# A short GpSimd instruction and a wait ahead of each scatter of two routings, in a kernel of graph layers, an LSTM and two expert layers

## The chip, the cores and the metric

The kernel runs on one core of a Trainium2 chip. The metric is the device time of one execution in microseconds (us). The core has five engines with a queue of instructions each: TensorE (PE), VectorE (DVE), ScalarE (ACT), GpSimd (POOL) and SyncE (SP, which here only starts DMAs). Engines wait for one another by semaphores alone.

## What is computed

The input `x` is 32 x 256 x 128 in fp32, 8192 tokens of 128 features, with a 256 x 256 adjacency matrix. Four residual layers follow one another, each behind a layer norm:

```python
x = x + _L0_gnn_ref(_layernorm(x), adj, adj, ...)    # gated graph layer
x = x + _L0_ffn_ref(_layernorm(x), ...)              # top-1 of 8 experts, behind a shared hidden layer of 512
x = x + _L1_gnn_ref(_layernorm(x), adj, ...)         # two graph layers, then LSTMs over windows of 1 to 4 nodes
x = x + _L1_ffn_ref(_layernorm(x), ...)              # top-2 of 8 experts, 341 wide
```

In the second layer `assign = argmax(probs)` chooses one expert for each token; in the fourth `top_k(probs, 2)` chooses two. The kernel computes only the chosen experts, so the tokens have to be brought into the order of the experts and back.

## The kernel before

The 8192 tokens are 64 tiles of 128 tokens. All layers run in one program with a stream of instructions written out for each engine.

**First routing (second layer).** The router runs over all 64 tiles (`b1_up`, PE line 1179, with ACT L828). In three batches (`PARTS`: 24, 24 and 16 tiles) DVE works out for each token its row in `sorted_in`, a DRAM array ordered by experts, and writes it to `dest_i` (L1767). `scatter_b(b)` on POOL then sends one indirect DMA per tile (L676), 128 rows of 512 bytes each. The first batch waits per scatter for an early count of the router's matmuls, which has been reached by then; the second batch waits likewise and from its 11th scatter on for the expert loop's matmuls (`b2_h`), 5 for each 8 scatters; the third for 7 of them for each 8 scatters.

**Expert loop (`b2_pe`).** The sorted rows are handled in groups of four tiles, 18 in all, with two buffers. SP loads a group (`b2_load`, L501); PE transposes it (L1142) one group ahead, computes the hidden layer (`hidden`, L1150, four matmuls of 512 columns, each counted in `b2_h`) and the chosen experts' output (L1291). SP may load groups 0 to 3 once the first batch of scatters has landed, groups 4 to 7 after the second, the rest after the third. `gather` on POOL (L704) brings the results back, also with one indirect DMA per tile. Ahead of each stands `pause()`, a memset of a 128 x 1 tile that nothing reads (L659), followed by a wait of POOL for the end of that memset.

**LSTM and second routing.** The third layer is done in two halves. In the second half the LSTM steps run (PE L1415 and L1422, ACT L975 and L983, DVE L2074 to L2090) while DVE works out the places for the first half's tokens; `scatter_d` then sends two indirect DMAs per tile for 32 tiles (L685, rows of 528 bytes into `expert_in`), each tile waiting for a step of the LSTM (`l_h`). When all 64 have landed, SP loads the first groups of the last expert stage (L537), and PE transposes them (L1432).

**Last stage.** PE computes the experts (L1442, L1452), POOL sends 64 more scatters for the second half's tokens (`rows_in`, L729) and 136 stores of result rows (`rows_home`, L710), and DVE adds the rows up. Neither of these has a pause.

POOL's order is fixed: the three batches of `scatter_b`, the gathers, layer norm statistics, `scatter_d`, then the last stage.

Of the kernel before, what the change touches and what calls it, by code (L numbers as in the profile page):

```python
# [55 lines left out]
def build(nc, x, adj_t, bias_io, gate_w, gate_b, w1, b1, wg, bg, wd, bd, g0_w, g0_b, g1_w, g1_b, wih_t, whh_t, bih, bhh,  # L56
# [30 lines left out]
    with ExitStack() as ctx:  # L87
# [494 lines left out]
        def _(pool):  # L582
            def step(ins):
                ins.then_inc(pool_step, 1)
                n_pool[0] += 1
                pool.wait_ge(pool_step, n_pool[0])
# [71 lines left out]
            def pause():  # L658
                step(pool.memset(pause_p[:, :], 0.0))  # L659

            def scatter_b(b):
                pool.wait_ge(rb.dest, b + 1)
                if b == 0:
                    pool.wait_ge(zeroed, ZEROS)
                lo, hi = PARTS[b]
                for t in range(lo, hi):
                    i = t - lo
                    if b == 0:
                        pool.wait_ge(rb.h, KH * NG // 2 + 7 + 3 * i // 4)
                    elif b == 1 and i < 10:  # L670
                        pool.wait_ge(rb.h, KH * NG - 9 + i)
                    elif b == 1:
                        pool.wait_ge(b2_h, 1 + 5 * (i - 10) // 8)
                    else:
                        pool.wait_ge(b2_h, 10 + 7 * i // 8)
                    pool.indirect_dma_start(  # L676
                        out=sorted_in, out_offset=bass.IndirectOffsetOnAxis(ap=dest_i[:, 0, t:t + 1], axis=0),
                        in_=XN[:, t, :], in_offset=None).then_inc(s_scat[0][b], 16)

            def scatter_d():  # L680
                pool.wait_ge(rd.dest, 1)
                for t in range(NH):
                    pool.wait_ge(l_h, NL + SCATTER_STEP + (NL - 1 - SCATTER_STEP) * t // NH)
                    for k in range(2):
                        pool.indirect_dma_start(  # L685
                            out=expert_in, out_offset=bass.IndirectOffsetOnAxis(ap=dest_i[:, k, t:t + 1], axis=0),
                            in_=XR[:, t, :], in_offset=None).then_inc(s_scat[1][0], 16)
# [26 lines left out]
            for b in range(len(PARTS)):  # L714
                scatter_b(b)
# [17 lines left out]
            for k in range(NGH // 2):  # L733
                t_finish(0, k, 2)
            scatter_d()
            for i in range(HOME_FIRST):
                if i in LN_AT:
# [1574 lines left out]
```

## Time and profile before

| | |
|---|---|
| median of 3 runs | 1147.16 us (1145.66 to 1150.82) |
| profiled execution | 1153.07 us, its span 1151.2 us |
| PE busy | 1024.0 us, 89% |
| ACT, DVE, POOL busy | 619.4 (54%), 600.0 (52%), 483.7 us (42%) |
| mean granted TensorE clock | 0.956 of full speed |
| software DMA queue (POOL's) | 12544 packets, 25.98 MB, 6.8% of 16 engines |

Times in rows are counted from the start of the span. "Busy" leaves out waits, branches and the issue of DMAs by SP. For an indirect DMA the busy time is POOL's part, the making of its descriptors, not the transfer. "Issue" is time in which an engine waited for nothing that the profile shows; "remote" or "another core or an unknown queue" is a release whose source the profile could not find.

### The profile page before, as it was taken

How to read it: one execution, taken by the hardware profiler on the slowest of the kernel's cores; microseconds unless marked ns; L12 is line 12 of the kernel's file. 1: busy time of each engine (PE TensorE's matmuls, PEld its weight loads, DVE VectorE, ACT ScalarE, POOL GpSimd, SP SyncE). 2: the span in 40 equal slices, each digit the busy share in tenths (PEclk: the TensorE clock that was granted, in tenths of full speed). 3: DMA queues.
4: the chain of work that ended last, by engine and by line, in shares of the span. 5: the costliest groups of instructions: out<-in, count | busy, mean ns of one | idle time of the engine just before them, and what ended most of it. 6: DMA issues, size and time to landing. Idle time of an engine off the chain costs nothing.

```text
span 1151.2 us, 17554 instructions
## 1 busy us (share of the span) xinstructions
PE 1024.0 (89%) x5432; PEld 715.8 (62%) x5433; DVE 600.0 (52%) x1829; ACT 619.4 (54%) x1158; POOL 483.7 (42%) x703
## 2 busy tenths in 40 slices
PE   5799967899989899999999996999897799989993
PEld 2344423577667544654785463448897798889893
DVE  6977874411174265655756753336464523333365
ACT  4678843444333485655338754456776555545551
POOL 5852274531634420000220075533536666656652
PEclk9899988799998999999999997999998999999997
DMA  9940012232323030000000011121122222212547
GB/s 274 365 193 1 1 50 69 87 97 70 97 71 86 28 116 0 1 1 0 1 1 1 1 48 40 41 61 31 43 62 65 64 81 65 82 62 66 189 164 223
DMA packets 79876, 86.28 MB, mean 75 GB/s; under 512 B 10115, under 2 KB 65971, under 8 KB 79027
## 3 DMA queue, kind: packets, MB, share of 16 engines
q1 hardware_dynamic: 67250, 59.28, 16.2%
q0 software_dynamic: 12544, 25.98, 6.8%
q8 instruction: 44, 0.72, 0.3%
q14 instruction: 38, 0.30, 0.1%
HBM read 40.64 MB, written 44.58 MB: 74 GB/s over the span
## 4 chain that ended last, share of the span: by engine, by line
PE 67%; DVE 13%; ACT 6%; issue 6%; another core or an unknown queue 6%; DMA 1%; ACTq 1%; POOL 1%; DVEq 0%; POOLq 0%; SPq 0%
PE bank L1415 17%; PE bank L1442 14%; PE bank L1422 9%; PE bank L1452 5%; PE bank L1150 4%; PE bank L1291 3%; PE bank L1331 2%; PE bank L1179 2%; PE bank L1359 2%; ACT sb_whh_sb L955 1%; PE bank L1348 1%; PE bank L1320 1%; PE bank L1340 1%; DVE sb_R L1542 1%
## 5 line engine op out<-in xcount | busy, mean ns | idle before, releaser
L1415 PE MATMUL bank<-sb_R,sb_wih_sb 128*128 128x512 f32 (+2 forms) x504 | 203.0, 554 | 15.0 <-ACT sb_R L975 7.6
L975 ACT ACTIVATE sb_R<-bank,sb_lb_sb 128x512 f32<-128x512 f32 (+2 forms) x252 | 153.2, 634 | 93.4 <-PE bank L1422 67.4
L710 POOL DMA_INDIRECT expert_out<-sb_R,sb_slot_row x136 | 132.6, 975 | 115.9 <-ACT sb_R L998 45.5
L2243 DVE TENSOR_TENSOR sb_R<-sb_R,bank 114x384 f32<-114x384 f32 x136 | 75.3, 554 | 181.9 <-ACT sb_R L1032 107.3
L1415 PEld LDWEIGHTS bank<-sb_R,sb_wih_sb 128*128 128x128 f32 x504 | 97.1, 194 | 113.7 <-issue 82.8
L1032 ACT ACTIVATE sb_R<-bank 114x384 f32<-114x384 f32 x136 | 66.4, 489 | 142.5 <-PE bank L1442 102.8
L1442 PE MATMUL bank<-sb_xt,sb_wih_sb 128*114 128x128 f32 x792 | 103.5, 282 | 22.8 <-issue 7.2
L1452 PE MATMUL bank<-sb_BIG,sb_R 114*128 x816 | 115.7, 278 | 0.7 <-DVE sb_R L2172 0.5
L1442 PEld LDWEIGHTS bank<-sb_xt,sb_wih_sb 128*114 128x114 f32 x792 | 94.1, 184 | 28.6 <-issue 25.4
L1422 PE MATMUL bank<-sb_R,sb_whh_sb 128*128 128x512 f32 (+2 forms) x288 | 111.1, 529 | 0.0
L685 POOL DMA_INDIRECT expert_in<-sb_R,sb_dest_i x64 | 64.4, 1007 | 105.1 <-DVE sb_dest_i L1767 62.7
L1452 PEld LDWEIGHTS bank<-sb_BIG,sb_R 114*128 114x128 f32 x816 | 103.5, 194 | 0.9 <-issue 0.9
L1442 PE MATMUL bank<-sb_xt,sb_whh_sb 128*114 128x128 f32 x792 | 98.6, 274 | 5.7 <-ACT sb_wih_sb L955 5.6
L614 POOL TENSOR_TENSOR sb_ln_p<-sb_ST 128x8 f32<-128x8 f32 (+2 forms) x15 | 3.3, 222 | 222.6 <-DVE sb_ST L1657 162.5
L1442 PEld LDWEIGHTS bank<-sb_xt,sb_whh_sb 128*114 128x114 f32 x792 | 91.2, 178 | 8.1 <-issue 7.1
L899 ACT ACTIVATE sb_R<-bank,sb_b_sb 128x512 f32<-128x512 f32 x72 | 47.9, 688 | 83.9 <-PE bank L1150 75.0
L1422 PEld LDWEIGHTS bank<-sb_R,sb_whh_sb 128*128 128x128 f32 x288 | 54.7, 190 | 50.5 <-issue 35.6
L676 POOL DMA_INDIRECT sorted_in<-sb_R,sb_dest_i x64 | 62.9, 983 | 44.2 <-issue 16.9
L729 POOL DMA_INDIRECT expert_in<-sb_R,sb_dest_i x64 | 61.9, 967 | 41.1 <-PE bank L1442 16.2
L1291 PE MATMUL bank<-sb_BIG,sb_R 128*128 x576 | 69.8, 279 | 8.3 <-issue 4.3
L1179 PE MATMUL bank<-sb_xt,sb_w_sb 128*128 128x512 f32 x128 | 68.5, 632 | 9.1 <-ACT sb_R L828 9.1
L1291 PEld LDWEIGHTS bank<-sb_BIG,sb_R 128*128 128x128 f32 x576 | 67.6, 195 | 9.4 <-issue 9.4
(308 smaller groups left out, 1690.9 us busy)
## 6 DMA issues: line engine op xcount, KB each, us to landing
sb_XS<-expert_in SPq DMA_DIRECT2D x17, 528.0 KB
expert_in<-sb_R SPq DMA_DIRECT2D x17, 512.0 KB, 6.1
sb_R<-expert_out SPq DMA_DIRECT2D x6, 1024.0 KB, 8.3
sorted_in<-sb_R SPq DMA_DIRECT2D x9, 512.0 KB, 5.4
sb_XS<-sorted_in SPq DMA_DIRECT2D x18, 256.0 KB
sorted_out<-sb_R SPq DMA_DIRECT2D x18, 256.0 KB
sb_X<-x SPq DMA_DIRECT2D x8, 512.0 KB, 7.4
out<-sb_X SPq DMA_DIRECT2D x6, 512.0 KB
```

Of the source, the lines that this page charges most:

```text
L676: pool.indirect_dma_start(out=sorted_in, out_offset=bass.IndirectOffsetOnAxis(ap=dest_i[:, 0, t:t + 1], axis=0), in_=XN[:, t, :], in_offse ...
L685: pool.indirect_dma_start(out=expert_in, out_offset=bass.IndirectOffsetOnAxis(ap=dest_i[:, k, t:t + 1], axis=0), in_=XR[:, t, :], in_offse ...
L710: pool.indirect_dma_start(out=expert_out, out_offset=bass.IndirectOffsetOnAxis(ap=slot_row[:, i:i + 1], axis=0), in_=yd[i // 8 % RING][:, ...
L975: act.activation(gb[s][k][:, 0:c], bank[4 * s + k][:, 0:c], funcs[k], bias=lb_sb[:, (p - 1) * GATES + k:(p - 1) * GATES + k + 1]).then_inc ...
L1032: act.activation(sl[j % 2][0:HC, :], bank[2 + 2 * (j % 2)][0:HC, 0:KU * P], ACT.Silu).then_inc(d2_silu, 1)
L1179: pe.matmul(bank[2 + c % 2][:, :], w1_sb[:, c * P:(c + 1) * P], xt[b // 2 % 2][:, b % 2 * BANK:(b % 2 + 1) * BANK], start=True, stop=True) ...
L1291: mm = pe.matmul(bank[6 + u][:, j * P:(j + 1) * P], Ht[u][:, c, j * P:(j + 1) * P], wd_sb[:, c, bass.ds(er[j] * D, D)], start=(c == 0 and ...
L1415: mm = pe.matmul(bank[4 * s + k][:, 0:c].rearrange("p (w b) -> p w b", b=GH), wih_sb[:, p - 1, k * P:(k + 1) * P], xin, start=True, stop=( ...
L1422: pe.matmul(bank[4 * s + k][:, 0:c], whh_sb[:, p - 1, k * P:(k + 1) * P], hst[s][:, 0:c], start=False, stop=True).then_inc(l_g, 1)
L1442: mm = pe.matmul(bank[2 + 2 * (j % 2) + part][0:HC, c * P:(c + 1) * P], weights_of(i)[:, part * UP + c * HC:part * UP + (c + 1) * HC], xt[ ...
L1452: mm = pe.matmul(bank[6 + j % 2][:, 0:D], hm[j % 2][0:HC, c * P:(c + 1) * P], down_sb[0:HC, bass.ds(expert * (KU * D) + c * D, D)], start= ...
L2243: dve.tensor_tensor(hm[j % 2][0:HC, :], sl[j % 2][0:HC, :], bank[3 + 2 * (j % 2)][0:HC, 0:KU * P], ALU.mult).then_inc(d2_m, 1)
```

## The change

`pause()` is called ahead of each of the 64 scatters of the first routing and of each of the 64 scatters of `scatter_d`. The gates stay where they are, ahead of the pause. `pause()` itself is unchanged.

```diff
@@ scatter_b
                         pool.wait_ge(b2_h, 1 + 5 * (i - 10) // 8)
                     else:
                         pool.wait_ge(b2_h, 10 + 7 * i // 8)
+                    pause()
                     pool.indirect_dma_start(
                         out=sorted_in, out_offset=bass.IndirectOffsetOnAxis(ap=dest_i[:, 0, t:t + 1], axis=0),
                         in_=XN[:, t, :], in_offset=None).then_inc(s_scat[0][b], 16)
@@ scatter_d
                 for t in range(NH):
                     pool.wait_ge(l_h, NL + SCATTER_STEP + (NL - 1 - SCATTER_STEP) * t // NH)
                     for k in range(2):
+                        pause()
                         pool.indirect_dma_start(
                             out=expert_in, out_offset=bass.IndirectOffsetOnAxis(ap=dest_i[:, k, t:t + 1], axis=0),
                             in_=XR[:, t, :], in_offset=None).then_inc(s_scat[1][0], 16)
```

What it calls:

```python
def step(ins):
    ins.then_inc(pool_step, 1)
    n_pool[0] += 1
    pool.wait_ge(pool_step, n_pool[0])

def pause():
    step(pool.memset(pause_p[:, :], 0.0))
```

## Rows read from the trace of the kernel before

**Rows 1.** The page: shares of the chain that ended last, by engine.
```profile
PE 67%; DVE 13%; ACT 6%; issue 6%; another core or an unknown queue 6%; DMA 1%; ACTq 1%; POOL 1%; DVEq 0%; POOLq 0%; SPq 0%
```

**Rows 2.** The chain in order of time, 164 to 176: start, us, what.
```profile
164.30 9.78 issue
```

**Rows 3.** Timeline, 142 to 185: start, us, engine, line, instruction [idle before <- releaser].
```profile
142.56 1.31 POOL L676 DMA_INDIRECT sorted_in<-sb_R,sb_dest_i  x1 [4.20 <-DVE sb_dest_i L1767]
...
173.13 0.95 POOL L676 DMA_INDIRECT sorted_in<-sb_R,sb_dest_i  x1 [0.30 <-issue]
...
174.08 0.69 ACT L828 ACTIVATE sb_R<-bank,sb_b_sb 128x512 f32<-128x512 f32 x1 [9.21 <-issue]
...
175.37 14.15 SPq L501 DMA_DIRECT2D sb_XS<-sorted_in  x3
...
184.95 0.97 POOL L676 DMA_INDIRECT sorted_in<-sb_R,sb_dest_i  x1 [10.86 <-DVE sb_dest_i L1767]
```

**Rows 4.** The chain in order of time, 194 to 210.
```profile
197.69 1.45 issue
```

**Rows 5.** Timeline of PE, 186 to 250: the first groups of the expert loop.
```profile
188.52 0.60 PE L1142 MATMUL bank<-sb_ident,sb_XS 128*128 128x128 f32 x4
189.90 3.67 PE L1150 MATMUL bank<-sb_xt,sb_w_sb 128*128 128x512 f32 x8 [0.78 <-DVE sb_LG L1611]
...
218.21 3.60 PE L1150 MATMUL bank<-sb_xt,sb_w_sb 128*128 128x512 f32 x8
...
225.65 3.60 PE L1150 MATMUL bank<-sb_xt,sb_w_sb 128*128 128x512 f32 x8
229.09 0.60 PE L1142 MATMUL bank<-sb_ident,sb_XS 128*128 128x128 f32 x4
```

**Rows 6.** Windows: stretch, length, busy PE PEld DVE ACT POOL, PEclk, DMA, GB/s.
```profile
164.30:174.80 10.50, 1.69 (x4) 0.39 (x3) 2.86 (x15) 1.26 (x2) 7.65 (x8) 0.76 0.16 55
194.30:209.00 14.70, 6.45 (x37) 4.47 (x35) 4.69 (x21) 4.17 (x7) 9.17 (x10) 0.71 0.19 62
...
690.00:705.10 15.10, 3.97 (x11) 1.73 (x9) 2.92 (x6) 3.57 (x8) 7.95 (x8) 0.68 0.12 40
250.00:280.00 30.00, 30.00 (x178) 22.01 (x177) 3.54 (x16) 13.15 (x21) 0.00 (x0) 1.00 0.24 70
...
140.00:150.00 10.00, 9.82 (x49) 4.27 (x48) 9.65 (x33) 7.76 (x16) 5.91 (x6) 1.00 0.11 35
```

**Rows 7.** Timeline, 684 to 712, around the end of POOL's stream.
```profile
699.55 0.96 POOL L685 DMA_INDIRECT expert_in<-sb_R,sb_dest_i  x1 [0.31 <-issue]
703.21 1.83 ACT L975 ACTIVATE sb_R<-bank,sb_lb_sb 128x336 f32<-128x336 f32 x4 [8.32 <-remote]
```

**Rows 8.** The page's groups: instructions xcount | busy, mean ns | idle before.
```profile
L710 POOL DMA_INDIRECT expert_out<-sb_R,sb_slot_row x136 | 132.6, 975 | 115.9 <-ACT sb_R L998 45.5
...
L729 POOL DMA_INDIRECT expert_in<-sb_R,sb_dest_i x64 | 61.9, 967 | 41.1 <-PE bank L1442 16.2
```

**Rows 9.** Timeline of POOL in the gathers, around 299.
```profile
299.36 0.11 POOL L659 MEMSET sb_pause_p<- 128x1 f32 x1
299.75 0.94 POOL L704 DMA_INDIRECT sb_R<-sorted_out,sb_dest_i  x1 [0.27 <-POOL sb_pause_p L659]
```

**Rows 10.** Timeline, 766 to 782: the start of the last expert stage.
```profile
771.45 1.00 SPq L537 DMA_DIRECT2D sb_XS<-expert_in  x2
...
778.42 1.04 PE L1432 MATMUL bank<-sb_ident,sb_XS 128*128 128x128 f32 x8
```

**Rows 11.** Timeline, 299 to 309, in the gathers.
```profile
305.83 2.42 ACT L899 ACTIVATE sb_R<-bank,sb_b_sb 128x512 f32<-128x512 f32 x4 [7.48 <-remote]
...
306.66 2.71 PE L1291 MATMUL bank<-sb_BIG,sb_R 128*128 x11 [2.51 <-ACT sb_R L899]
```

**Rows 12.** Timeline, 859 to 882 and 908 to 921, in the last stage.
```profile
873.22 2.88 PE L1442 MATMUL bank<-sb_xt,sb_wih_sb 128*114 128x128 f32 x12 [5.78 <-DVE sb_R L2243]
...
919.85 1.38 PE L1442 MATMUL bank<-sb_xt,sb_wih_sb 128*114 128x128 f32 x5 [5.04 <-issue]
```

## The prediction

> **What bounds the kernel now.** I read the page's chain first: TensorE (PE) is 67% of it, and GpSimd (POOL), whose queue the change lengthens, is 1% [rows 1]. Counted by work alone, the change touches nothing that decides. So I looked in the chain in order of time and in the timeline for PE time lost while POOL sends scatters. Three stretches stand out.
>
> Stall A, 164.3 to 174.1 us, in the first batch of 24 scatters of the first routing. The chain gives 9.78 us to "issue" [rows 2]. ACT L828 stood 9.21 us and started at 174.08; no releaser is seen. POOL's last scatter of this batch ended at 173.13 + 0.95 = 174.08 as well [rows 3].
>
> Stall B, from 197.7 us, in the second batch: the chain shows gaps between single matmuls, the first of 1.45 us [rows 4], and then half clock; the granted clock of the whole stretch is 0.71 [rows 6]. Its cost is best read from the groups of the expert loop. An undisturbed group takes 225.65 - 218.21 = 7.44 us. Group 0 starts at 189.90, so with an estimated 0.4 us for the ranking matmuls between, group 2 is due at 189.90 + 2 x 7.44 + 0.4 = 205.2. It started at 218.21 [rows 5]: B costs 13.0 us.
>
> Stall C, up to 703.2 us, in the scatters of the second routing: ACT L975 waits 8.32 us on something unnamed and then does four pieces in a row. POOL's stream had ended 2.70 us before, at 699.55 + 0.96 = 700.51 [rows 7].
>
> With what the lower clock takes near A and C (granted 0.76 and 0.68 there [rows 6]; an estimate of 0.8 and 1.7 us) the three are worth 10 + 13 + 10 = 33 us, 3% of the span. All lie under scatters that follow one another without a gate. Where POOL issues nothing PE is gapless, as in 250 to 280 us [rows 6]. An added pause is small beside this; what decides is whether it touches these stalls.
>
> **The change part by part.** It adds 64 + 64 memsets of 128x1 and as many waits for their ends to POOL's stream; nothing is removed or moved. The gathers carry the same pair, so its price can be read. In a stream a scatter takes 0.95 us after 0.30 of idle, 1.26 us with rounding [rows 3]; a paused gather takes 0.11 (memset) + 0.27 (idle) + 0.94 (DMA) = 1.33 us by its starts [rows 9]. That is +0.063 us (1.326 less 1.263) per scatter, 8 us of POOL time over 128. Where POOL first waits for another engine, that wait now sits at the memset, and some 0.3 us come on top once.
>
> Queued behind each pause are its scatter and all later ones; SP waits for a batch's completion before it loads expert input, and PE waits for that.
>
> First batch: 24 x 0.063 + 0.3 = 1.8 us later. SP's first load goes out at 175.37, 1.29 us after the last scatter [rows 3], and PE takes the data at 188.52 [rows 5]; the router's work covers it. If A goes, PE comes about 10 us earlier, and with an estimated 2 us for the data the cover falls from 11 to 1 us, less the 1.8: a wait of at most 1 us.
>
> Second batch: POOL waited 10.86 us for its destinations, to 184.95 [rows 3], because DVE crawled through A as well. Without A they come before batch 1 can start, and POOL is the limit: it starts at 174.1 + 1.8 = 175.9, needs 24 x 1.33 = 31.8, to 207.7, then 1.3 to SP's load and about 2 for the data: 211. PE's transposes for group 4 stood at 229.09 [rows 5]; less A and B they are due at 206.1. So 5 us are taken back by a new wait of PE for group 4 (unpaused 3.5 us, by the same sum with 1.5 less). These 5 include the 1 us above, since both end in the same place.
>
> Third batch: its gates let 8 scatters go per 7 of PE's matmul quarters; PE paces it. Nothing.
>
> Second routing: the gates of the LSTM steps pace the later scatters. After the last one SP loads at 771.45, and PE needs the data at 778.42, after its last recurrent matmuls [rows 10]. Two late pauses, 0.4 us, are hidden in these 7 us less about 2 of loading; 0.4 if that cover is gone.
>
> So as the kernel stands the pauses themselves cost PE between 0 and 2 us.
>
> **Do they stop the stalls?** No row shows a paused scatter. The nearest are the 64 paused gathers. They have one stall, D: ACT's 7.48 us of idle time end at 305.83, and PE stood 2.51 us [rows 11]. At a spacing of 1.33 us about five pauses fell into D and did not end it. The unpaused indirect DMAs are the 128 scatters here, 64 later ones and 136 stores of rows [rows 8], 328 in all, with A, B, C and two more stalls in the last stage, where PE stood 5.78 and 5.04 us [rows 12]. So the frequency, 5 in 328, is that of the gathers, 1 in 64. The price is not: 44 us in 328 are 0.13 us each, against 2.5 in 64, 0.04. Bounds: the stalls vanish (-33 us), or they stay and stretch with their streams (+1.8 for A, +1.4 for B, +0.4 at the end of the second routing: +3.6). I take the gathers' frequency, because they carry the very edit: two stalls in 128 scatters. Their price I double to 5 us each, because the first batch has no gate that would cut a stall short.
>
> [...]
>
> **Sum.** -33 + 5 (new wait for group 4) + 10 (remaining stalls) + 0.4 = -17.6 us. The profiled execution took 1153.07 us, of which 1151.2 is its span, and lies 5.9 above the median of 1147.16. The sum gives 1135.5 against its own time, and 1129.6, say 1130, against the median, which I predict.
>
> **The rivals.**
> 1. The pauses do nothing to the stalls. A ends with POOL's batch to the hundredth, C 2.7 us after its stream: they last as long as the stream does, a pause leaves POOL as busy as before, and D went on through five of them. Then +3.6: 1150.8. Against it: the lower price in the gathers.
> 2. Slower: the stall of the first batch sets in sooner. A set in at 164.87, 22.3 us after the batch began at 142.56 [rows 3]; B 12.7 us after its own began at 184.95. This batch has no gate for 24 scatters, so a stall holds until its end. If the new spacing lets it start at 12.7 us, it is 9.6 us longer: 9.6 + 3.6 = 13.2, 1160; 1155 if half of it falls on idle time of PE. It decides from the point where ACT's gap begins before the 17th scatter. For it: B. Against: nothing in the trace but A's own onset.
> 3. One stall of three goes. B alone, with group 4's wait already half paid: 13 less 5 and 2 for the stretched A, 6 us; C alone, 10 less 3.2. About 1141.
> 4. The memsets of the first batch wait for DVE, which is busy 9.65 of 10 us there, in 33 instructions of 0.29 us [rows 6], where in the gathers it has less to do. One such instruction per pause is 24 x 0.29 = 7 us on the first batch and so on group 4's wait: 1137 for 1130. The Trainium skill has it that GpSimd and certain DVE instructions lock each other out of a port pair that they share (SBUF — State Buffer, section SBUF: two separate sides); the 0.11 us memset [rows 9] shows no such wait.
>
> The edit will do what it says, since 64 such pairs are in the trace. It does not wait for a DMA's landing: the memset starts as soon as the DMA instruction before it has left the engine.
>
> **Chances.** Forecast 0.39, its own range 1120 to 1140; rival 1 0.27; rival 2 0.18; rival 3 0.10; rival 4 0.04; 0.02 for stalls that merely change places at equal cost. Half a per cent, about what a measurement of this kernel can tell from no change, is 5.7 us: 1141.4 to 1152.9. Faster is the forecast, rival 4 and half of rival 3: 0.48. Same is rival 1, the other half and most of the rest: 0.33. Slower is rival 2 and a little of the rest: 0.19. The range, 1121 (one stall fewer left, group 4 nearly on time) to 1157, leaves out 0.08 below and the upper half of rival 2.
>
> **What would show it.** A spacing of 1.33 us between scatters shows the price. ACT's gap at 165 gone and group 2 of the expert loop 20 us sooner show the cure; PE idle ahead of group 4's transposes shows the new wait. "Issue" or an unnamed wait of 8 us or more in the chain, ending with POOL's stream in a paused batch, refutes me. I would be wrong in size if stalls come or go in the unpaused scatters and row stores of the last stage, since all of these shift in time.

## The result: 1.8% faster

| | before | after |
|---|---|---|
| median | 1146.37 us (1145.66 to 1150.82, 6 runs) | 1126.74 us (1122.69 to 1131.68, 6 runs) |
| ratio | | 0.9823, 95% interval 0.9801 to 0.9845 |
| profiled execution | 1153.07 us, span 1151.2 | 1131.68 us, span 1129.8 |
| mean granted clock | 0.956 | 0.964 |

The forecast was 1130 (1121 to 1157). The profiled executions differ by 21.4 us. Where these went is read from landmarks on TensorE (PE) that both traces have, each the start of a row of the timeline:

| PE reaches | before | after | gain of the stretch |
|---|---|---|---|
| group 0 of the expert loop | 189.90 | 193.89 | -4.0 |
| group 2 of the expert loop | 218.21 | 211.48 | +10.7 |
| first matmul after the expert loop (before's L1331) | 346.50 | 341.02 | -1.3 |
| second half of the LSTM layer | 609.85 | 604.34 | 0.0 |
| first transposes of the last stage (before's L1432) | 778.42 | 756.12 | +16.8 |
| end of the span | 1151.2 | 1129.8 | -0.9 |

In this pair of profiles two stretches carry all of it: the second batch of the first routing (stall B) and the second routing (stall C). One profile is one execution; a second profile of the change, e9_change below, repeats C's part and not B's. From the first added call on, the lines of after stand one or two further down than those of before.

The price of a pause, in POOL's timeline of after, 152 to 155 us (start us, duration, engine, line, operation, idle before it and what ended it); it answers to [rows 3, 9]:

```profile
151.88 0.96 POOL L677 DMA_INDIRECT sorted_in<-sb_R,sb_dest_i  x1 [0.28 <-issue]
152.84 0.11 POOL L659 MEMSET sb_pause_p<- 128x1 f32 x1
153.23 0.96 POOL L677 DMA_INDIRECT sorted_in<-sb_R,sb_dest_i  x1 [0.28 <-issue]
```

153.23 - 151.88 = 1.35 us from scatter to scatter, 0.087 more than the 1.263 of before; 0.063 had been forecast.

**Stall A is still there.** The chain in order of time, 169 to 191 us (start, duration, step), and PE's and ACT's timeline at the same place, answering to [rows 2, 3]:

```profile
169.15 6.43 issue
...
180.70 4.21 another core or an unknown queue
...
187.03 3.57 another core or an unknown queue
```

```profile
168.02 1.13 PE L1181 MATMUL bank<-sb_xt,sb_w_sb 128*128 128x512 f32 x2
174.93 0.60 ACT L836 ACTIVATE sb_R<-bank 128x512 f32<-128x512 f32 x1 [6.45 <-remote]
175.58 1.11 PE L1209 MATMUL bank<-sb_ident,sb_R 128*128 128x128 f32 x4 [6.43 <-issue]
```

ACT stands 6.45 us and PE 6.43 us. ACT goes on at 174.93, shortly before POOL's last scatter of the batch leaves the engine (174.06 + 1.05 = 175.11). PE's hole is 2.4 us shorter than the 8.83 us that PE lost in A before. Two holes of PE follow, under the second batch (2.01 us up to 185.58 and 2.48 us up to 191.28). They were not there before, and they take back more than that: group 0 starts 4.0 us later.

**Stall B is gone in this profile.** PE's timeline, 192 to 228 us, answering to [rows 5]:

```profile
193.89 5.86 PE L1152 MATMUL bank<-sb_xt,sb_w_sb 128*128 128x512 f32 x8 [0.78 <-ACT sb_xt L755]
...
204.04 3.60 PE L1152 MATMUL bank<-sb_xt,sb_w_sb 128*128 128x512 f32 x8
...
211.48 3.60 PE L1152 MATMUL bank<-sb_xt,sb_w_sb 128*128 128x512 f32 x8
...
223.72 0.60 PE L1144 MATMUL bank<-sb_ident,sb_XS 128*128 128x128 f32 x4
```

Groups 1 and 2 are 7.44 us apart, an undisturbed group. Group 0 takes 5.86 us for its eight matmuls instead of 3.60: the granted clock was 0.76 from 186 to 200 us, after the idle time ahead of it. The last row is group 4's transposes, without any wait ahead of them.

**Stall C is gone, and at its end PE waits for POOL.** Busy time in three stretches of the second routing, after, then the same stretches of before (from : to, length, busy us and instructions of PE, PEld, DVE, ACT and POOL, granted clock, DMA share, GB/s):

```profile
610.00:660.00 50.00, 50.00 (x120) 22.61 (x119) 39.78 (x87) 38.50 (x62) 1.94 (x4) 1.00 0.01 2
660.00:700.00 40.00, 40.00 (x136) 25.57 (x135) 21.34 (x44) 26.28 (x52) 31.77 (x56) 1.00 0.14 46
700.00:750.00 50.00, 50.00 (x126) 23.60 (x125) 21.23 (x33) 29.70 (x47) 39.37 (x69) 1.00 0.15 48
```

```profile
660.00:700.00 40.00, 33.96 (x104) 19.50 (x102) 18.18 (x40) 18.03 (x33) 28.10 (x28) 0.94 0.14 46
700.00:750.00 50.00, 42.20 (x112) 22.98 (x113) 17.85 (x32) 25.91 (x48) 28.27 (x29) 0.88 0.12 39
```

PE is never idle under 64 paused scatters; before it lost 6.0 and 7.8 us in these two stretches and got a clock of 0.94 and 0.88. Then the end of the stream, in the chain of after:

```profile
748.21 0.97 POOL expert_in L687
...
749.57 2.38 DMA expert_in<-sb_R,sb_dest_i
751.97 4.02 DMA sb_XS<-expert_in
755.98 0.14 issue
756.12 0.64 PE bank L1434 x4
```

PE was done at 750.30 + 3.60 = 753.90 and waits 2.22 us for its data. In before the chain of this place ran through PE.

### The profile page after: what moved, and what is told of

Same layout as the page of the kernel before. It is cut to its first block, busy times and chain, and to the rows that moved or that the text cites. A ratio compares the mean times of both kernels' runs of the same rounds, so it can differ in the third digit from the quotient of the medians.

```text
span 1129.8 us, 17682 instructions
## 1 busy us (share of the span) xinstructions
PE 1019.6 (90%) x5432; PEld 714.9 (63%) x5433; DVE 600.5 (53%) x1829; ACT 617.1 (55%) x1158; POOL 500.0 (44%) x831
## 4 chain that ended last, share of the span: by engine, by line
PE 65%; DVE 13%; ACT 7%; another core or an unknown queue 6%; issue 5%; DMA 2%; POOL 1%; ACTq 1%; DVEq 0%; POOLq 0%; SPq 0%
PE bank L1417 16%; PE bank L1444 14%; PE bank L1424 8%; PE bank L1454 4%; PE bank L1293 3%; PE bank L1181 3%; PE bank L1152 2%; PE bank L1333 2%; PE bank L1361 2%; ACT sb_whh_sb L957 2%; PE bank L1118 1%; PE bank L1322 1%; PE bank L1350 1%; ACTq L951 1%
## 5 line engine op out<-in xcount | busy, mean ns | idle before, releaser
L1417 PE MATMUL bank<-sb_R,sb_wih_sb 128*128 128x512 f32 (+2 forms) x504 | 197.8, 543 | 1.2 <-issue 1.2
L659 POOL MEMSET sb_pause_p<- 128x1 f32 x192 | 21.6, 112 | 168.9 <-DVE sb_dest_i L1769 66.4
L731 POOL DMA_INDIRECT expert_in<-sb_R,sb_dest_i x64 | 62.1, 970 | 40.4 <-PE bank L1444 17.3
L687 POOL DMA_INDIRECT expert_in<-sb_R,sb_dest_i x64 | 66.5, 1039 | 19.4 <-POOL sb_pause_p L659 11.8
```

Source lines behind the costliest of these rows:

```text
L687: pool.indirect_dma_start(out=expert_in, out_offset=bass.IndirectOffsetOnAxis(ap=dest_i[:, k, t:t + 1], axis=0), in_=XR[:, t, :], in_offse ...
L731: pool.indirect_dma_start(out=expert_in, out_offset=bass.IndirectOffsetOnAxis(ap=dest_i[:, k, t:t + 1], axis=0), in_=XR[:, t - NH, :], in_ ...
L1417: mm = pe.matmul(bank[4 * s + k][:, 0:c].rearrange("p (w b) -> p w b", b=GH), wih_sb[:, p - 1, k * P:(k + 1) * P], xin, start=True, stop=( ...
```

## The experiments

What I set out to tell apart: is it the pause's wait for an end that cures (and not the memset, nor the wider spacing of the scatters), which of the two places brings what, would more or fewer pauses do better, and what is left in the first batch.

One thing has to be said ahead of them, since without it no number below can be read. The kernel before took 1146 to 1161 us (medians) on three of the six occasions on which it ran, and 1063 to 1065 us on three others. Each kernel is compared with runs of before made on the same occasion. I call the first occasions *stalling* and the second *calm*; the section after this one shows the difference. It doesn't look like one chip against another: under the same chip number, 6, the kernel before took 1156.82 us on one occasion and 1064.80 on another.

Medians are in us. Each ratio and its interval are those on record for the occasion; they differ by up to 0.3% from the quotient of the two medians beside them, which for e4_no_wait would be 1.0037.

| kernel | occasion | before | this | ratio, 95% interval |
|---|---|---|---|---|
| e1_first_only | stalling | 1156.82 | 1150.30 | 0.9946 [0.9917, 0.9976] |
| e2_second_only | stalling | 1156.82 | 1143.69 | 0.9862 [0.9822, 0.9901] |
| e3_everywhere | stalling | 1156.82 | 1142.97 | 0.9874 [0.9821, 0.9928] |
| e4_no_wait | stalling | 1156.82 | 1161.15 | 1.0008 [0.9977, 1.004] |
| e9_change | stalling | 1160.81 | 1139.35 | 0.9829 [0.9798, 0.9861] |
| e10_mixed | stalling | 1160.81 | 1160.27 | 0.9995 [0.9972, 1.0017] |
| e5_none | calm | 1063.04 | 1062.02 | 0.9995 [0.9983, 1.0006] |
| e6_two_no_wait | calm | 1063.04 | 1064.87 | 1.0004 [0.9992, 1.0015] |
| e7_every_other | calm | 1063.04 | 1063.24 | 1.0004 [0.9993, 1.0014] |
| e8_double_first | calm | 1063.04 | 1072.11 | 1.0084 [1.0065, 1.0103] |
| e11_wide | calm | 1064.80 | 1080.45 | 1.0153 [1.0126, 1.0179] |
| e12_apart | calm | 1064.26 | 1078.41 | 1.0130 [1.0109, 1.0152] |

### One place alone: e1_first_only and e2_second_only

```diff
@@ e1, from the change: scatter_d
                     for k in range(2):
-                        pause()
                         pool.indirect_dma_start(
@@ e2, from the change: scatter_b
-                    pause()
                     pool.indirect_dma_start(
```

> Pauses ahead of the 64 scatters of the first routing alone. Theory P (the pause itself makes stalls of other engines rarer and shorter): the expert loop's group 2 starts near 211 us as with the whole change, the second routing keeps its stall of 8 us or more at ACT L975, and the time is the kernel before less the 5.4 us by which the graph layers start sooner: 1141 us. Theory R (any shift of POOL's timing moves the stalls about, the pause has no effect of its own): the first routing looks as with the whole change, since nothing ahead of it differs, but the second one, which starts 5 us sooner, may lose its stall as well: anywhere from 1127 to 1141.

> Pauses ahead of the 64 scatters of the second routing alone. Theory P: stalls A and B stay as they were (group 2 of the expert loop at 218 us), the LSTM part from the first gates' matmuls to the transposes of the last stage takes 151.6 us as with the whole change instead of 168.4, and the time is 1146.4 less some 16: 1130 us. Theory R: the scatters start 5 us later than with the whole change, and a stall is as likely as it was before: 1130 to 1146.

Measured: 0.9946 and 0.9862. The product is 0.981, and the change has 0.9823 on another occasion: within the intervals the two places add up. The second is worth 16 us, the first 6. For e1 I had expected group 2 of the expert loop near 211 us, as in the first profile of the change; it starts at 215.27, and between 197 and 209 us PE again does single matmuls with gaps. Stall B is there in spite of the pauses. Stall C, without pauses, is there too, in e1's ACT timeline:

```profile
678.54 0.47 ACT L984 ACTIVATE sb_R<-sb_R 128x336 f32<-128x336 f32 x1
688.06 0.54 ACT L976 ACTIVATE sb_R<-bank,sb_lb_sb 128x336 f32<-128x336 f32 x1 [9.05 <-remote]
```

### More pauses: e3_everywhere

```diff
@@ rows_home
                 pool.wait_ge(d2_yo, i + 1)
+                pause()
                 pool.indirect_dma_start(
@@ rows_in
                     pool.wait_ge(d2_h, IN_AT[b - 1] + 5 * i // 8)
+                    pause()
                     pool.indirect_dma_start(
```

> The pause also ahead of the 64 scatters and 136 row stores of the last stage. Theory P: the two stalls of the last stage (PE idle 4.7 and 4.3 us with the change) go or shrink, 200 pauses of 0.09 us are hidden behind PE's gates but for 0.4 us at the very end: 1126.7 - 8 + 0.5 = 1119 us. Theory R: the stalls change places, 1122 to 1135. If POOL becomes the bound in the last stage, where its stores follow PE closely: slower than 1127 with PE waiting for buffers.

Measured: 0.9874; its interval just holds the change's ratio. 200 more pauses bring no gain, where 8 us had been expected. In the last stage of this kernel the two large stalls of PE are smaller (3.48 and 3.72 us), but shorter waits have appeared, two of them for DVE's additions:

```profile
923.70 1.54 PE L1446 MATMUL bank<-sb_xt,sb_wih_sb 128*114 128x128 f32 x12 [2.29 <-DVE sb_R L2247]
...
948.79 2.56 PE L1446 MATMUL bank<-sb_xt,sb_whh_sb 128*114 128x128 f32 x12 [2.23 <-DVE sb_R L2247]
```

From the first transposes of the last stage to the end of DVE's last addition it takes 379 us, against 376 to 378 in e1, e2 and e4 of the same occasion and 371 and 373 in the change's two profiles. What the smaller stalls gave was lost within the last stage.

### The memset without the wait: e4_no_wait

```diff
-            pause_p = sb("pause_p", [P, 1])
+            pause_p = sb("pause_p", [P, 130])
...
+            def touch():
+                n_touch[0] += 1
+                pool.memset(pause_p[:, n_touch[0]:n_touch[0] + 1], 0.0)
@@ scatter_b and scatter_d, from the change
-                    pause()
+                    touch()
```

> The same 128 memsets, each to a column of its own, without the wait for their ends. If the wait is what helps (POOL's queue stands empty once per scatter), the stalls are back: 1143 to 1148 us. If the added time between two DMAs helps (spacing), scatters start 1.3 us or more apart and the time is that of the change, 1127. If the pairing of any other instruction between two DMAs helps, also 1127, at a spacing near the old 1.26.

Measured: 1.0008, no gain at all. The 128 memsets are there, but the scatters stand 1.26 us apart as in before: the memset lies in the 0.30 us in which POOL idles between two DMAs anyway.

```profile
151.34 0.96 POOL L683 DMA_INDIRECT sorted_in<-sb_R,sb_dest_i  x1 [0.19 <-issue]
152.30 0.12 POOL L665 MEMSET sb_pause_p<- 128x1 f32 x1
152.61 0.96 POOL L683 DMA_INDIRECT sorted_in<-sb_R,sb_dest_i  x1 [0.19 <-issue]
```

The stall of the second routing is back, in ACT's timeline:

```profile
691.79 0.47 ACT L991 ACTIVATE sb_R<-sb_R 128x336 f32<-128x336 f32 x1
701.32 1.83 ACT L983 ACTIVATE sb_R<-bank,sb_lb_sb 128x336 f32<-128x336 f32 x4 [9.06 <-remote]
```

So another instruction between two scatters doesn't help; what the change adds beyond it is the wait, and with it 0.087 us of spacing. Which of these two cures is the next question.

### Two memsets without the wait: e6_two_no_wait, and e10_mixed with it

```diff
             def touch():
+                for _ in range(2):
                     n_touch[0] += 1
                     pool.memset(pause_p[:, n_touch[0]:n_touch[0] + 1], 0.0)
@@ e6: touch() in scatter_b and scatter_d; e10: in scatter_d only, and in scatter_b
+                    if i % 2 == 0:
+                        pause()
```

> The change with two memsets, each into its own column, ahead of each scatter of the two routings, and no wait for them. The scatters should come about 1.39 us apart, further than the change's 1.35. Theory P (the wait for an end cures): stalls A to C stay, ratio to before 0.998 to 1.004. Spacing theory (anything that puts 1.35 us or more between two scatters cures): the stall of the second routing is gone, ratio 0.980 to 0.988.

> The change with the pause ahead of every other scatter only in the first routing, and in the second routing with two memsets and no wait ahead of each scatter (which come 1.38 us apart then, no closer than with the pause). On a chip where before stalls: theory P (the wait for an end cures) expects the hole of about 8 us in ACT and PE in the second routing to be there, and the whole at 0.992 to 1.00 of before; the spacing theory expects no hole there, and 0.980 to 0.988. In the first routing, theory P1 (a wait now and then is enough) expects the holes after 185 us gone, P2 (each scatter needs its own) expects them back. On a chip where before does not stall: 0.999 to 1.003.

e6 fell on a calm occasion and tells nothing of the cure. e10 ran beside the change on a stalling one: 0.9995. The stall of the second routing is there, PE standing 6.27 and 7.23 us, and ACT 9.07 us:

```profile
717.66 0.49 ACT L993 ACTIVATE sb_R<-sb_R 128x352 f32<-128x352 f32 x1
...
722.49 0.95 POOL L695 DMA_INDIRECT expert_in<-sb_R,sb_dest_i  x1 [0.16 <-issue]
723.44 0.15 POOL L666 MEMSET sb_pause_p<- 128x1 f32 x2
723.75 0.96 POOL L695 DMA_INDIRECT expert_in<-sb_R,sb_dest_i  x1 [0.16 <-issue]
...
727.22 0.54 ACT L985 ACTIVATE sb_R<-bank,sb_lb_sb 128x336 f32<-128x336 f32 x1 [9.07 <-issue]
```

The same rows show that my expectation was wrong in its premise: two memsets take 0.15 us together, and the scatters still stand 1.26 us apart, not 1.38. So e10 repeats e4 with two memsets; it does not set spacing against wait. For every other scatter in the first routing it shows group 0 at 189.8 and the first matmul after the expert loop at 345.15, where the change beside it has 187.8 and 342.78: not better than a pause each time, and with one profile of each no more can be said. PE's hole in the first batch is 7.90 us there against 5.27 in e9.

### The change again: e9_change

> The change itself, unaltered, on another day's chip. The kernel before has taken 1156.8 us on one chip and 1063.0 us on a second, where its routings show no stall of ACT and PE. Theory P+C (the pause removes stalls that only some chips have): where before takes 1145 us or more, ratio 0.980 to 0.985; where before takes about 1063 us, there is nothing to remove, GpSimd's stream of 64 in the second routing takes 64 x 0.085 = 5.4 us longer and reaches past PE's work, ratio 0.999 to 1.004. Rival (the pause gains by something else than the stalls, such as the order in which data arrives): ratio 0.98 to 0.99 on either.

Measured: 0.9829 against the first comparison's 0.9823. The gain repeats on another stalling occasion. The second routing shows the same picture as in the first profile, with no hole of PE above 2 us, and the two stalls of the last stage are there again (4.72 and 5.02 us). The first routing differs. Group 0 starts at 187.84, so the 4.0 us that the first profile lost ahead of it are not a property of the change. Stall A is there (PE 5.27 us, up to 171.07), and it does not end with the batch: ACT goes on 5.6 us before POOL's last scatter has left the engine (174.99 + 0.96).

```profile
170.33 0.69 ACT L830 ACTIVATE sb_R<-bank,sb_b_sb 128x512 f32<-128x512 f32 x1 [3.69 <-remote]
...
174.99 0.96 POOL L677 DMA_INDIRECT sorted_in<-sb_R,sb_dest_i  x1 [0.28 <-POOL sb_pause_p L659]
```

And stall B is there, in spite of the pauses. PE's timeline, 195 to 213 us, and the window around it:

```profile
195.95 0.59 PE L1152 MATMUL bank<-sb_xt,sb_w_sb 128*128 128x512 f32 x1
197.36 0.59 PE L1152 MATMUL bank<-sb_xt,sb_w_sb 128*128 128x512 f32 x1 [0.81 <-issue]
198.83 1.42 PE L1152 MATMUL bank<-sb_xt,sb_w_sb 128*128 128x512 f32 x2 [0.88 <-issue]
...
212.80 3.60 PE L1152 MATMUL bank<-sb_xt,sb_w_sb 128*128 128x512 f32 x8
```

```profile
200.00:215.00 15.00, 11.77 (x47) 7.46 (x47) 6.95 (x27) 2.91 (x5) 10.35 (x19) 0.77 0.20 62
```

From group 1 at 195.95 to group 2 it takes 16.85 us, where an undisturbed group takes 7.44. So which stalls go in the first routing has to be read from all profiles of stalling occasions. Times are in us; the fourth column is from the start of group 0 to that of group 2:

| kernel | pause in the first routing | PE's hole in the first batch | groups 0 to 2 | group 0 | first matmul after the expert loop |
|---|---|---|---|---|---|
| before | none | 8.83 | 28.3 | 189.90 | 346.50 |
| e2 | none | 10.90 | 25.5 | 194.39 | 349.80 |
| e4 | memset, no wait | 9.16 and 2.03 | 27.1 | 193.34 | 350.78 |
| after | each | 6.43 | 17.6 | 193.89 | 341.02 |
| e9 | each | 5.27 | 25.0 | 187.84 | 342.78 |
| e1 | each | 6.88 | 26.0 | 189.29 | 344.67 |
| e3 | each | 5.79 | 26.5 | 187.46 | 343.98 |
| e10 | every other | 7.90 | 25.4 | 189.79 | 345.15 |

Without any stall (e5 below) groups 0 to 2 take 17.1 us. So B is gone in one of four profiles with a pause ahead of each scatter, and hardly shorter than without pauses in the other three. What is common to the four is a shorter A. Within one occasion (e1 and e3 against e2 and e4) group 0 starts 4 to 7 us sooner and the expert loop ends 5 to 7 us sooner: what the pauses gained there in the first routing was won ahead of group 0. The second routing is clear: stall C is in all four profiles without the wait (before, e1, e4, e10) and in none of the four with it (after, e2, e3, e9).

### No pauses at all, and every other: e5_none and e7_every_other

```diff
@@ e5, from before: gather
-                    pause()
@@ e7, from the change: scatter_b, scatter_d
+                    if i % 2 == 0:
                         pause()
+                        if k == 0:
                             pause()
```

> The kernel before without its own pauses: no memset and wait ahead of the 64 gathers either. Theory P (a stream of GpSimd's indirect DMAs without a wait for an end stalls the other engines): the gathers' stream, which now runs between about 245 and 400 us, begins to stall them as well; two to four new holes of 5 to 10 us in ACT and PE, the kernel 10 to 30 us slower than before (ratio 1.01 to 1.025). Theory G (only scatters, which write to device memory, stall the others): no new holes, ratio 0.999 to 1.003.

> The change with the pause ahead of every other scatter only (the even ones of a batch in the first routing, the first of each tile's two in the second). The stream of 64 in the second routing gets 32 times 0.085 = 2.7 us shorter. Theory P1 (a wait now and then is enough): no stall in the second routing, PE at its end 2 us sooner, ratio to before 0.978 to 0.984. Theory P2 (each scatter needs its own): one of the two scatters of a pair finds another in work, stalls return at least in part, ratio 0.988 to 1.00.

Both fell on a calm occasion: 0.9995 and 1.0004. With not one pause in the program there is no stall in it. So "a stream of indirect DMAs stalls the other engines" can't be true of the program alone. What the gathers' pauses bring on a stalling occasion stays open.

### Longer spacing and no wait: e11_wide and e12_apart; two pauses: e8_double_first

```diff
+            def wide():
+                for _ in range(3):
+                    if n_wide[0] >= 4:
+                        pool.wait_ge(pool_step, n_pool[0] - 3)
+                    lo = 1 + 80 * (n_wide[0] % 4)
+                    pool.memset(pause_p[:, lo:lo + 80], 0.0).then_inc(pool_step, 1)
+                    n_pool[0] += 1
+                    n_wide[0] += 1
@@ e11, e12: scatter_d
-                        pause()
+                        wide()
@@ e8, e11: scatter_b
                     pause()
+                    if b == 0:
+                        pause()
```

> The change with two pauses, one behind the other, ahead of each of the first batch's 24 scatters, where the stall in GpSimd's first stream is still there (6.4 us of PE in the changed kernel). Theory T (the first batch stalls since one pause leaves too little room): the hole at about 169 us goes, 4 to 6 us less than the change, ratio to before 0.974 to 0.980. Theory O (the first batch's stall has another cause than scatters close behind each other): it stays, and the batch ends 24 times 0.37 = 9 us later; ratio 0.981 to 0.990.

> The change with three memsets of 128x80 instead of one of 128x1 ahead of each scatter of the second routing, and no wait for their end (only one for the end of the memset four back, long past); and with two pauses instead of one ahead of each of the first batch's 24 scatters. In the second routing the three memsets should keep the scatters 1.4 to 1.5 us apart, more than the pause does (1.35). Where before stalls: theory W (the wait for an end cures) expects ACT and PE to stall there for 6 to 9 us as before; the spacing theory expects no stall. In the first batch theory T (one pause leaves too little room) expects the hole of PE at about 165 us (5.3 to 6.4 us with one pause) gone, theory O (its cause lies elsewhere) expects it there. The whole by W and O: 0.995 to 1.005 of before; by the spacing theory and T: 0.978 to 0.985. Where before does not stall, neither shows, and the whole is at 1.008 to 1.015.

> First routing as in the change; in the second routing three memsets of 128x80 ahead of each scatter, without a wait for their end, which keep the scatters 1.53 us apart (the pause keeps them 1.35 apart). The kernel before has taken about 1157 us in two of the calls so far, with stalls in both routings, and about 1064 us in two others, without any. Where it stalls: theory W (the wait for an end cures) expects the hole of 6 to 9 us in ACT and PE in the second routing to be there, the whole 0.998 to 1.008 of before; the spacing theory expects no hole and 0.986 to 0.992, since the stream of 64 scatters ends 7 us later than PE. Where it does not stall, the first routing tells what the pause costs there (group 0 of the first routing starts 0 to 3 us later than with no pause, by 24 x 0.085 = 2 us), and the whole is 1.008 to 1.012.

All three fell on calm occasions, so the question they were made for, spacing or wait, is not answered. They do give prices, and all three are slower than before, by 0.8 to 1.5%. In e12 the scatters of the second routing stand 1.53 us apart, the stream ends at 743.1, and PE waits for its end:

```profile
737.52 1.88 PE L1435 MATMUL bank<-sb_R,sb_whh_sb 128*128 128x512 f32 x4
748.59 1.73 PE L1445 MATMUL bank<-sb_ident,sb_XS 128*128 128x128 f32 x7 [9.19 <-DMA sb_XS<-expert_in]
```

In e8, whose second routing is the change's, the stream ends at 735.9, 7.2 us earlier, and PE waits 2.14 us, 7.05 less. In e5 it ends at 724.5 and PE doesn't wait. So in these three, past the point where PE is ready, a microsecond of POOL's stream is a microsecond of the kernel.

```profile
741.26 1.06 PE L1436 MATMUL bank<-sb_ident,sb_XS 128*128 128x128 f32 x8 [2.14 <-DMA sb_XS<-expert_in]
```

The first batch likewise. Group 0 starts at 179.2 without pauses (e5), 182.5 with one (e12), 185.6 and 186.0 with two (e8, e11): +3.3 and +6.4 to 6.8 us. In e12 PE waits 3.44 us for the load ahead of group 0, where it waited 0.84 us in e5, and 2.21 us ahead of group 4, where it waited 3.00 in e5:

```profile
180.60 1.09 PE L1155 MATMUL bank<-sb_ident,sb_XS 128*128 128x128 f32 x4 [3.44 <-DMA sb_XS<-sorted_in]
...
213.24 0.66 PE L1155 MATMUL bank<-sb_ident,sb_XS 128*128 128x128 f32 x4 [2.21 <-DMA sb_XS<-sorted_in]
```

The change itself was not run on a calm occasion. An estimate from e8: it took 1072.11 us, with the change's second routing; the first matmul after the expert loop stands at 330.78 there and at 325.96 in e12, which has the change's first routing; 1072.1 - 4.8 = 1067.3, or 1.004 of before.

## Why the forecast came out, point by point

**What bounds the kernel** was right on every occasion that stalls: PE, with three stretches lost under POOL's scatters. That these stretches belong to the kernel was wrong. The same stretch of the first routing, 164 to 175 us, in after and then in e5_none on a calm occasion (columns as above); before had a clock of 0.76 there [rows 6]:

```profile
164.00:175.00 11.00, 5.15 (x18) 1.50 (x16) 9.73 (x39) 2.30 (x5) 8.78 (x17) 0.81 0.14 49
```

```profile
164.00:175.00 11.00, 11.00 (x48) 3.90 (x46) 9.69 (x40) 6.90 (x11) 7.54 (x8) 1.00 0.16 55
```

The program is the same up to the pauses, the scatters are as long (0.96 us) and in e5 closer (1.26 us apart against 1.35), the DMA engines are as busy (0.14 and 0.16), and PE does 48 records of work instead of 18. The same holds for the last stage, 850 to 950 us, again after and e5_none:

```profile
850.00:950.00 100.00, 87.51 (x723) 85.18 (x724) 44.19 (x142) 58.48 (x117) 63.00 (x65) 0.93 0.24 70
```

```profile
850.00:950.00 100.00, 100.00 (x911) 100.00 (x911) 42.72 (x130) 63.34 (x119) 75.82 (x80) 1.00 0.32 92
```

From the first transposes of the last stage to the end of DVE's last addition, e5_none takes 324.7 us, the change 370.9 and before 370.0. No profile of before was kept from a calm occasion, so e5_none (0.9995 of it) stands in for it. Of the 90 us between before on a stalling occasion and e5_none, some 45 lie in this last stage, 24 ahead of the first matmul after the expert loop (346.5 against 322.8) and the remaining 22 between the two, in the second routing above all. The prediction counted 33 as there to be won; the other 57 were lost where its view of the three holes didn't look, most of it in the last stage, at 0.23 to 0.24 of DMA share against 0.32. What causes that loss no run shows.

**The price of a pause:** 0.063 forecast, 0.087 measured. The term was too small by over a quarter because it set a paused gather against an unpaused scatter: the gathers do stand 1.33 us apart, but a gather's DMA takes 0.94 us and a scatter's 0.96, before and after, and the idle time is 0.28 instead of 0.27. POOL's time for it is 11 us instead of 8.

**Stall A, -10 forecast, +4.0 measured** up to group 0, and -4 to -7 within one occasion (e1 and e3 against e2 and e4). This step failed: A does not go. The prediction took the frequency of the gathers, one stall in 64, as that of any paused stream; but A is in all four profiles with a pause each time (5.3 to 6.9 us of PE) and in e10. The pause shortens it: without the wait it takes PE 8.8 to 11.2 us. That A ended "with POOL's batch to the hundredth", as rival 1 had it, was chance in one profile: ACT goes on 5.6 us ahead of the batch's end in e9, 2.6 us ahead of it in e1, and 2.9 us behind it in e2. What decides its end is open; e8 was to try two pauses on it and met no stall.

**Stall B, -13 forecast, -10.7 measured** from group 0 to group 2; the rest is lower clock in group 0. This hit is luck. In e9, the same kernel, the stretch takes 25.0 us and not 17.6, and in e1 and e3 26.0 and 26.5, against 25.5 to 28.3 without the pauses. The pauses do not reliably stop B. The first routing as a whole still came out 5 to 7 us shorter, in the first pair at B's place and within the later occasion at A's.

**Stall C, -10 forecast, -16.8 measured,** net of a new wait. This is the step that held in every profile. The hole itself was mis-sized: the prediction took the 8.32 us of ACT, but PE lost 6.0 + 7.8 = 13.8 us in 660 to 750 us and ran at 0.94 and 0.88 of its clock in both stretches. The windows by stage would have shown it. Nor had POOL's stream ended at 700.51: its next scatter stood 6.58 us, up to 707.09, for DVE L2087, and the 64th left at 770.12. So C did not last "as long as the stream does", as rival 1 had it; here the stream stood and waited for a step of the LSTM.

**Remaining stalls in the paused streams, 2 x 5 = 10 forecast.** In the first profile it is A with 6.4 us and two holes behind it with 4.5; in e9 it is A with 5.3 and B with some 8.

**The new wait for group 4, 5 us forecast, 0 measured.** It needed A gone. With PE late by its own stall POOL's second batch was early enough. On calm occasions, where nothing holds PE up, the step is right in kind: with the change's first routing (e12) PE waits 3.44 us for group 0 and 2.21 for group 4, 5.65 together; without pauses (e5) 0.84 and 3.00, where 3.5 had been reckoned.

**The end of the second routing, 0 to 0.4 forecast, 2.2 measured.** The step had 2 us for the data's way; the rows give 2.38 for the scatter's landing and 4.02 for the load. And it left POOL's stream paced by the LSTM steps: without C these come sooner, POOL doesn't catch up, and its 64 x 1.35 = 86 us (657.87 to 750.64 in the trace) become the bound. The margin is thin: in e9 the stream ends at 753.09, PE is ready at 760.01, and no wait is left.

So the sum, -17.6 forecast and -19.6 (medians) or -21.4 (profiles) measured, is right to 2 to 4 us because its errors cancel. Against the landmarks of the first pair it counted on 14 us of gain at A and 2 at B that did not come. The other way it missed 7 us of gain in the second routing, its last wait included, charged 5 for group 4 that were not due, and set 10 aside for remaining stalls, which the landmark of A already holds. Losses of 1.3 us behind group 2 and 0.9 in the last stage it had at nothing.

**The rivals.** Rival 1 (pauses do nothing) holds for B in three of four profiles, for A only in that it stays, and not for C. Rival 2 (A sets in sooner) did not happen: ACT's idle time begins at 168.48 in the change (174.93 - 6.45) and at 166.64 in e9 (170.33 - 3.69), against 164.87 in before. Rival 3 (one stall of three goes, C alone, about 1141) is nearest to what e9 shows of the mechanism, though not in size: the first pair has 1126.7, since C was worth 17 us and not 10. Rival 4 (memsets wait for DVE) has nothing for it: the memsets of the first batch take 0.11 us beside a busy DVE, the longest of all 192 takes 0.25. The Trainium skill states a lock between GpSimd and some DVE instructions (SBUF — State Buffer, section SBUF: two separate sides); no memset of this trace was held up by more than the 0.14 us that lie between the two.

**What is shown and what isn't.** Shown: the wait together with its 0.087 us of spacing stops C, in four profiles of four, where the memset alone and two memsets leave it. A is shorter in all four than in the three without the wait, but with one execution each. Not shown: that the pauses stop B, and whether it is the wait or the spacing that works. Not known at all: what stalls ACT, PE and DVE on some occasions. It isn't the program's doing alone (e5_none), one chip number stands on both kinds of occasion, and the traces name no releaser for it. Nor is it the lack of a pause: the gathers, paused in all kernels but e5, show their stall D (2.5 to 2.8 us of PE, ending between 301 and 311 us) in all eight profiles of stalling occasions and in none of the six of calm ones. The Trainium skill warns that semaphore increments at a high rate from one engine can deadlock another, and would have kernels space dense increments that come from several engines (VectorE: DVE Perf Modes, section The TRN2 errata — SBUF-src ops pay a fixed extra latency per instruction). Nothing deadlocks here, since every stall ends by itself. The pause adds an increment to each scatter's own and helps all the same, and a calm occasion shows no stall at the same density; no run here bears the rule out as the cause.

No version beats both kernels everywhere. On stalling occasions the change has the lowest ratio of those run, though the intervals of e2 and e3 overlap with its own; on calm ones before and e5_none are, and pausing every other scatter costs nothing there (1.0004), though nothing shows that it cures.

## What to carry to other kernels

Before tuning against a stall for which the profile names no releaser, run the unchanged kernel on several occasions: here its time alone moves by 8% with the occasion, four times the change's gain. A wait for its own last instruction between GpSimd's indirect DMAs took a 14 us loss out of one stream at 0.09 us per DMA, where the same instruction without the wait gave nothing; in the two batches of the other routing it only shortened one stall and left the other in three profiles of four. Profile the changed kernel more than once before saying which stall went; price the wait against the end of the stream, since there each microsecond counts once the stall is gone. And size a stall by windows over the whole stage and its granted clock, not by its longest hole.

## What the hardware showed that I hadn't expected

- The same kernel takes 1063 to 1065 us or 1146 to 1161 us (medians of an occasion). On a calm occasion PE has no hole above 3.5 us from 140 us to the end (e5_none).
- A small memset between two indirect DMAs was free: one of 0.12 us or two of 0.15 us together left their spacing at 1.26 us. Only a wait for the memset's end (1.35 us) or 0.39 us of memsets (1.53 us) moved it.
- In a stalling second routing without the wait ACT's longest stop is 9.05 to 9.07 us in three kernels (e1, e4, e10) and 8.32 in before, each time at another place: up to 688, 701, 727 and 703 us. Shorter ones stand beside it (5.38 and 4.90 us in e10).
- The same kernel (after and e9_change), both times with no hole of PE above 2.3 us under the second routing's scatters, has stall B in one profile and not in the other.
